# Five TensorE signals per expert instead of ten, and the next expert's transposes behind all down products

## What is computed

```python
h = xf @ W_router + b_router                     # xf: (16384, 128), 32 experts
Sm = softmax(h)
G_ek, idx_ek = top_k(Sm.T, 512)                  # each expert takes its 512 best tokens
tokens = xf[idx_ek]
up = einsum('gjkh,ghf->gjkf', tok_g, W_up) + b_up     # 8 groups of 4 experts, 341 hidden
act = silu(up)
Eout = einsum('ekf,efh->ekh', act, W_down) + b_down
y = zeros.at[idx_ek].add(G_ek[..., None] * Eout)
```

## Time and profile before

| | us |
|---|---|
| median of 3 runs | 2606.75 |
| lowest, highest | 2601.83, 2608.33 |
| the profiled execution | 2612.21 |
| its span, first to last instruction | 2610.5 |
| TensorE busy | 2309.8 |
| VectorE busy | 1869.5 |
| ScalarE busy | 1692.1 |
| POOL busy | 1419.6 |

### The profile page before, as it was taken

One profiled execution on the slowest core, in us unless ns is written; L12 is line 12 of the kernel. 1 busy time (PEld: TensorE's weight loads), 2 busy tenths in 40 slices (PEclk: granted clock), 3 DMA queues, 4 the chain that ended last, 5 costly groups with the idle time before them and its releaser, 6 DMA issues.

```text
span 2610.5 us, 59252 instructions
## 1 busy us (share of the span) xinstructions
PE 2309.8 (88%) x16748; PEld 2017.1 (77%) x16764; DVE 1869.5 (72%) x8460; ACT 1692.1 (65%) x5249; POOL 1419.6 (54%) x1724
## 2 busy tenths in 40 slices
PE   4999977667777599999999999999999999999966
PEld 3877865444444499999999999899898999999855
DVE  4787767555445278888888887777778888788733
ACT  2777744122112287777787777888787888778744
POOL 6544100556556368778887774344443677447443
PEclk8999989888888799999999999999999999999988
DMA  2566686333333431111111126555554888468577
GB/s 74 195 234 209 222 213 97 101 109 122 112 118 117 131 94 50 46 46 43 48 51 46 46 75 170 156 161 163 156 154 110 242 231 243 133 194 243 147 218 226
DMA packets 357908, 361.96 MB, mean 139 GB/s; under 512 B 35603, under 2 KB 301692, under 8 KB 357584
## 3 DMA queue, kind: packets, MB, share of 16 engines
q1 hardware_dynamic: 321376, 272.95, 37.9%
q0 software_dynamic: 33472, 78.98, 9.2%
q10 hardware_dynamic: 2736, 6.25, 0.7%
HBM read 208.38 MB, written 144.00 MB: 135 GB/s over the span
## 4 chain that ended last, share of the span: by engine, by line
PE 64%; DVE 15%; issue 7%; another core or an unknown queue 4%; POOL 3%; ACT 3%; DMA 2%; ACTq 0%; SPq 0%; DVEq 0%; POOLq 0%
PE bank L2210 7%; PE bank L2289 6%; PE bank L2303 6%; PE bank L2221 5%; PE bank L2209 4%; PE bank L2236 4%; PE bank L2256 4%; PE bank L2238 4%; PE bank L2237 4%; PE bank L2264 3%; PE bank L2178 3%; PE bank L2084 2%; POOL rows L910 2%; PE bank L2162 2%
## 5 line engine op out<-in xcount | busy, mean ns | idle before, releaser
L948 POOL DMA_INDIRECT zbuf<-pc,kb x248 | 251.7, 1015 | 242.6 <-DVE pc L1863 189.7
L942 POOL DMA_INDIRECT spread_rows<-kb,pos x248 | 253.7, 1023 | 199.6 <-DVE pc L1863 105.1
L2210 PE MATMUL bank<-xT,gT 128*128 128x256 f32 x1024 | 306.1, 381 | 0.0
L1666 DVE COPY pr_place<-bank 128x384 f32<-128x384 f32 x512 | 281.6, 550 | 19.6 <-PE bank L2221 13.8
L1645 DVE TENSOR_REDUCE nmax<-bank 128x1 f32<-128x128 f32 x512 | 144.1, 282 | 195.8 <-PE bank L2210 108.9
L1153 ACT ACTIVATE pr_place<-bank,nmax 128x128 f32<-128x128 f32 x512 | 188.8, 369 | 136.4 <-DVE nmax L1646 122.6
L2303 PE MATMUL bank<-wvo_part,x_part 128*128 128x512 f32 x768 | 267.8, 457 | 1.1 <-ACT vo_place L1241 1.0
L1163 ACT ACTIVATE bank<-causal 128x384 f32<-128x384 f32 x512 | 253.4, 495 | 19.4 <-PE bank L2394 3.3
L2221 PE MATMUL bank<-ident,pr_place 128*128 128x128 f32 x1536 | 251.8, 273 | 9.9 <-DVE pr_place L1666 9.1
L2221 PEld LDWEIGHTS bank<-ident,pr_place 128*128 128x128 f32 x1536 | 196.9, 140 | 77.1 <-DVE pr_place L1659 14.5
L2289 PE MATMUL bank<-x_part,wqk_part 128*128 128x256 f32 x1536 | 245.8, 296 | 1.2 <-DVE x_part L1806 1.2
(11 more groups left out here) (363 smaller groups left out, 6570.2 us busy)
## 6 DMA issues: line engine op xcount, KB each, us to landing
pa<-bundle SPq DMA_DIRECT2D x196, 321.0 KB
table<-rows SPq DMA_DIRECT2D x96, 576.0 KB
rows<-table SPq DMA_DIRECT2D x192, 128.0 KB
wu_more<-bundle SPq DMA_DIRECT2D x65, 321.0 KB
kb<-spread_rows SPq DMA_DIRECT2D x248, 65.0 KB
junk<-zbuf SPq DMA_DIRECT2D x31, 512.0 KB
h3buf<-h SPq DMA_DIRECT2D x64, 128.0 KB
kb<-kb SPq DMA_DIRECT2D x31, 256.0 KB
```

What stands on the lines that cost most here:

```text
L942: pool.indirect_dma_start(out=spread_rows, out_offset=bass.IndirectOffsetOnAxis(ap=pos[:, k, j:j + 1], axis=0), in_=xr4s[g % 2][:, k, j], ...
L948: pool.indirect_dma_start(out=zbuf, out_offset=bass.IndirectOffsetOnAxis(ap=xu_at(t)[:, C + 1:XW].bitcast(U32), axis=0), in_=yu[:, t % YR] ...
L1666: dve.tensor_copy(prT[:, h % 2], t_bank(u)[:, 0:3 * P]).then_inc(prT_ready, 1)
L2210: pe.matmul(s2[:, P:3 * P], g[:, P:2 * P], xT3[:, p], start=False, stop=True, skip_group_check=True)\
```

## The change

- Up: one signal behind the third product; ScalarE waits once per expert.
- Down: chunks 0 and 1 lie in bank 4 and share a signal, chunks 2 and 3 in bank 7. Each pair waits for the weighing of the pair of the expert before in its bank. Weighing and SyncE's reload count two signals per expert.
- Rows: no signal (but for the first two experts and the last). `number(e + 2)` waits for the signal of bases(e + 3), which TensorE issues behind it. `rank(e + 3)` moves ahead of `number(e + 2)` on VectorE.
- TensorE's order for expert e becomes: turn_rows(e); two warm products; three ups; rows(e + 2); bases(e + 3); four warm products; down 0 to 3.
- The second layer's waits on the two counters take the new totals.

```diff
--- before.py
+++ after.py
@@ -205,7 +205,7 @@
             return w2d[x // 4][:, x % 4, k * C:(k + 1) * C]
 
         def down_at(c):
-            return bank[7 if c % 2 else 4][:, (c // 2) * P:(c // 2 + 1) * P]
+            return bank[7 if c // 2 else 4][:, (c % 2) * P:(c % 2 + 1) * P]
 
         def xg_at(g):
             return xg[:, g % 8] if g % 8 < 4 else xg_more[:, g % 8 - 4]
@@ -559,6 +559,7 @@
         FILLED = NK - 2
         DENSE = (ND + 1) * 2 * H1 + 13
         UPS, DOWNS = 3 * E0, TG * E0
+        UPS_TOLD, DOWNS_TOLD = E0, 2 * E0
         DENSE_STEP = 6
         DENSE_END = DENSE + DENSE_STEP * (E1 - 1) + 1
 
@@ -653,7 +654,7 @@
 
                 for q in range(2 if last else 4):
                     e, p = 4 * v + q, q % 2
-                    sp.wait_ge(dn_mm, TG * (e + 1))
+                    sp.wait_ge(dn_mm, 2 * (e + 1))
                     load_up(v + q // 2, p)
                     load_down(e + 2, p)
             for v in range(0, NU - 1):
@@ -1126,8 +1127,8 @@
                 act.wait_ge(bup_ready, 4 + 2 * v)
                 for q in range(4):
                     e = 4 * v + q
+                    act.wait_ge(up_mm, e + 1)
                     for k in range(3):
-                        act.wait_ge(up_mm, 3 * e + k + 1)
                         act.activation(ac[0:FCH[k], k], bank[1 + k][0:FCH[k], :], ACT.Silu, bias=bupg[0:FCH[k], k:k + 1])\
                             .then_inc(ac_ready, 1)
                     if not (last and q == 3):
@@ -1197,9 +1198,9 @@
 
             def dense_hidden(x):
                 for k in range(2):
-                    act.wait_ge(up_mm, UPS + 2 * x + k + 1)
+                    act.wait_ge(up_mm, UPS_TOLD + 2 * x + k + 1)
                     if x >= 2 and k == 0:
-                        act.wait_ge(dn_mm, DOWNS + x - 1)
+                        act.wait_ge(dn_mm, DOWNS_TOLD + x - 1)
                     act.activation(hd_at(x, k), bank[SBANK[k]][:, :], ACT.Relu, bias=b1T[:, x, k:k + 1]).then_inc(ac_ready, 1)
 
             def dense_gates_turned():
@@ -1543,7 +1544,10 @@
 
             def number(e, q, n):
 
-                dve.wait_ge(tab_mm, e + 1)
+                if 2 <= e < E0 - 1:
+                    dve.wait_ge(base_mm, e + 2)
+                else:
+                    dve.wait_ge(tab_mm, min(e + 1, 3))
                 n.done(dve.tensor_copy(tbase[:].rearrange("p (k c) -> p k c", k=2)[:, 0], bank[5][:, 0:2 * (P + 1)].rearrange("p (c t) -> p c t", c=2)[:, :, P]))
                 n.done(dve.tensor_copy(tbase[:].rearrange("p (k c) -> p k c", k=2)[:, 1], bank[6][:, 0:2 * (P + 1)].rearrange("p (c t) -> p c t", c=2)[:, :, P]))
                 n.wait()
@@ -1570,7 +1574,7 @@
             def weigh(e, p):
                 for c in range(TG):
                     acc = rows4[:, e % NTAB, c, ROW:ROWA]
-                    dve.wait_ge(dn_mm, TG * e + c + 1)
+                    dve.wait_ge(dn_mm, 2 * e + c // 2 + 1)
                     dve.scalar_tensor_tensor(out=acc, in0=down_at(c), scalar=gate[:, p, c:c + 1], in1=acc,
                                              op0=ALU.mult, op1=ALU.add).then_inc(ye_ready, 1)
 
@@ -1587,11 +1591,12 @@
                 n = Steps(dve, sel_step, pre + 4 * PER * v)
                 for q in range(4):
                     e, p = 4 * v + q, q % 2
+                    if not (last and q >= 1):
+                        rank(e + 3, n)
                     if not (last and q >= 2):
 
                         number(e + 2, (q + 2) % 4, n)
                     if not (last and q >= 1):
-                        rank(e + 3, n)
                         place(e + 3, n)
                     gates(e, p, n)
                     weigh(e, p)
@@ -1742,7 +1747,7 @@
                     dve.wait_ge(mask_ready, NG)
                 else:
                     dve.wait_ge(ye_ready, DOWNS + x)
-                dve.wait_ge(dn_mm, DOWNS + x + 1)
+                dve.wait_ge(dn_mm, DOWNS_TOLD + x + 1)
                 hh = h3[:].rearrange("p q j c -> p (q j) c")
                 for j in range(TG):
                     ins = dve.scalar_tensor_tensor(out=yd[:, j], in0=dense_bank(x)[:, j * C:(j + 1) * C], scalar=gmat[:, j, x:x + 1],
@@ -1751,7 +1756,7 @@
 
             def dense_biases():
                 dve.wait_ge(ye_ready, DOWNS + E1)
-                dve.wait_ge(dn_mm, DOWNS + E1 + 1)
+                dve.wait_ge(dn_mm, DOWNS_TOLD + E1 + 1)
                 dve.tensor_tensor(xeT[:], dense_bank(E1)[:, :], xeT[:], ALU.add).then_inc(ye_ready, 1)
 
             def gate_weights(g):
@@ -2131,7 +2136,8 @@
                 for c in range(TG):
                     o = bank[5 + c // 2][:, (c % 2) * (P + 1):(c % 2 + 1) * (P + 1)]
                     ins = pe.matmul(o, oneh[:, c * P:(c + 1) * P], tab[:], start=True, stop=True)
-                ins.then_inc(tab_mm, 1)
+                if e < 2 or e == E0 - 1:
+                    ins.then_inc(tab_mm, 1)
 
             pe.wait_ge(tq_ready, 1)
             for e in range(3):
@@ -2153,32 +2159,31 @@
             def serve(v, last):
                 for q in range(4):
                     e, p = 4 * v + q, q % 2
-                    if not (last and q >= 2):
-                        rows(e + 2)
+                    turn_rows(e)
                     stay_warm(3, 2)
                     pe.wait_ge(xeT_ready, e + 1)
                     pe.wait_ge(wup_in[p], 16 * (2 * v + q // 2 + 1))
                     for k in range(3):
-                        pe.matmul(bank[1 + k][0:FCH[k], :], wup[:, p, k * P:k * P + FCH[k]], xeT[:], start=True, stop=True)\
-                            .then_inc(up_mm, 1)
-                        if k == 1 and not (last and q >= 1):
-                            bases(e + 3)
-                    stay_warm(0, 3)
+                        ins = pe.matmul(bank[1 + k][0:FCH[k], :], wup[:, p, k * P:k * P + FCH[k]], xeT[:], start=True, stop=True)
+                    ins.then_inc(up_mm, 1)
+                    if not (last and q >= 2):
+                        rows(e + 2)
+                    if not (last and q >= 1):
+                        bases(e + 3)
+                    stay_warm(0, 4)
                     pe.wait_ge(ac_ready, 3 * e + 3)
                     pe.wait_ge(wdn_in[p], 48 * (2 * v + q // 2 + 1))
                     for c in range(TG):
-                        if c == 1 and not (last and q >= 1):
+                        if c == 2 and not (last and q >= 1):
                             pe.wait_ge(base_read, e + 4)
-                        if c == 2 and not (last and q == 3):
-                            turn_rows(e + 1)
-                        if TG * e + c >= 2:
-                            pe.wait_ge(ye_ready, TG * e + c - 1)
+                        if c % 2 == 0 and e >= 1:
+                            pe.wait_ge(ye_ready, TG * (e - 1) + c + 2)
                         for k in range(3):
                             m = FCH[k] + (k == 2)
                             ins = pe.matmul(down_at(c), ac[0:m, k, c * P:(c + 1) * P], wdn[0:m, p, k],
                                             start=(k == 0), stop=(k == 2))
-                        ins.then_inc(dn_mm, 1)
-            turn_rows(0)
+                        if c % 2:
+                            ins.then_inc(dn_mm, 1)
             serve(0, False)
             for v in range(1, NU - 1):
                 serve(v, False)
```

## The result

| | before | changed |
|---|---|---|
| median | 2607.54 us (4 runs) | 2654.01 us (4 runs) |
| lowest, highest | 2601.83, 2620.23 | 2644.88, 2664.47 |
| profiled execution | 2612.21 | 2664.47 |
| ratio, 95% interval | | 1.0171 [1.013, 1.0212] |

A forecast was written before the change was run, and what follows sets the result against it. A two-expert loop of waits bounds the expert stage. Leg 9.05 + 1.8 + 0.9 = 11.75, with 13.11 on POOL, gives period 12.43 against 13.19: 0.76 x 31 = 23.6 us gained, near 2583; range 2549 to 2609.

The forecast's parts named there:

- The bound and the loop of two legs: First layer's expert stage: a chain of waits over two experts, 13.84 us on TensorE plus 13.11 on POOL, sets the period.
- POOL leg: From first weighing of expert e to transposes of e+2, eight indirect transfers included: 13.11 us, expected unchanged.
- (1): Up products: three signals become one, so the first silu waits for all three; 1.7 us head start lost, cost 0.
- (2): Down products: four signals become two, pairs in one bank; first weighing waits 0.67 us longer, cost 0 under the same cover.
- VectorE's branch: Number, place and gate up to the first weighing, at 9.05 us; ends 1.0 after the silu and down branch at 8.05.
- (4): Rank before number, rows and bases behind the ups: third up product no longer held up; later index costs 0.
- (3): Transposes of e+1 move behind down product 3: last two products, weighings and scatters freed; e+1's chain needed them anyway.
- The lateness taken: Late signals on the TensorE leg: 0.5 us for transposes, 1.9 for base product, in three of four experts: 1.8 us.
- Prompt leg 9.05: From transposes to first weighing in the changed kernel, at full clock with prompt signals: 9.05 us.
- Half clock share kept at 24%: TensorE at half clock for today's share of the stage lengthens 3.9 us of work on the leg by 0.9 us.
- Slower: Rival: TensorE's own serial loop becomes the bound, 13.9 us per expert, +22 us, 2629 us; chance 0.14.
- Signals turn prompt: Rival: fewer TensorE signals no longer queue, period 11.1 to 12.1, gain 65 to 34 us, time 2542 to 2573; chance 0.18.

The follow-up runs named there:

- e4: The kernel before with only the signal counts and banks changed: one signal for three ups, two for four downs; ratio 1.0082 to before.
- e1: The changed kernel with the transposes put back between down products 1 and 2; ratio 0.9968 to before.
- e18: The changed kernel with a short break on POOL, a fill of 160 columns, ahead of scatter 2; ratio 0.9948 to before.
- e2: The kernel before with only the transposes moved behind down product 3; ratio 1.0102 to before.
- e8: The kernel before with a signal nobody waits for on each of the seven warm products per expert; ratio 1.0019 to before.
- e16: The changed kernel with each scatter replaced by a gather of the same rows into an idle tile, sums left out; one execution, 2622.80 us.
- e6: The changed kernel with six warm products instead of two between the transposes and the ups; ratio 1.0003 to before.
- e12: The kernel of e6 with six warm products instead of two also behind the downs, before the wait for the gather; ratio 1.0006 to before.
- e15: The changed kernel with a break on POOL, a fill of 1284 columns, ahead of scatter 2; ratio 0.9991 to before.

## Why the prediction was wrong

- **The bound and the loop of two legs**: right, but it closes over the even experts alone. Their leg is 16.2 us in the mean and their POOL leg 13.2, half the sum 14.7, against a measured period of 14.74. The odd experts have 10.0, where the prediction has both "alike"; their transposes follow TensorE's own downs, and their POOL leg of 19.3 sets nothing.
- **(1), (2) signals at cost 0 under VectorE's branch**: right only with the new order. Alone they cost 0.8% (e4).
- **(4) order**: right in sign. The predicted 2583 would have been -0.9% for all parts; the order alone gave -0.4%, with the signals -0.3% (e1).
- **(3) the transposes' move**: this failed, in two sentences. "What now stands behind them is expert e+1's own chain, which needed them anyway: 0" looked only at what waits for the transposes, not at what TensorE does behind them. In the kernel before twelve down matmuls followed at once and the copy came 0.15 us late in the mean; now only two warm products follow, and it came 2.46 us late, in 13 experts over 1 us, up to 9.5. In the even experts, which close the loop, that is 4.7 us, where 0.75 x 0.5, about 0.4, was taken. It is the largest addition to their leg of 16.2: 9.05 prompt, 4.7 for the held signal, and some 2.3 more than in odd experts for transposes and ups at the lower clock.
- **The lateness taken**, "0.5 and 1.9": the 1.9 stood on the base product's signal, the 0.5 on the transposes'. The trace has it the other way round. In expert 12 the base product ends at 650.79 and number starts at 650.84, and in the mean it starts 0.1 us behind; the transposes' signal is the late one, and so, in front of each of the 13 late copies, is the last down signal. The upper bound, "as late as the worst seen: 1.46 and 2.26", was no bound: the kernel before shows no signal in front of an idle TensorE in a long run of POOL's but the down signal of chunk 1, late by 2.9 us (725.17 to 728.06), and even that was counted as "the next 2 us behind it", a queue.
- **Prompt leg 9.05**: right where signals are prompt and the clock is full. The odd experts of e18 have 8.9, its even ones, behind the stand for the gather, 10.6.
- **Half clock share kept at 24%**: it rose to 36% (granted clock 0.82), as TensorE's stands grew (1.09 us of work in 9.60 in the window above, at 0.56). The term taken was 0.9 us; the 2.3 above stand against it.
- **Rivals.** "Slower" had the sign but not the mechanism: it has TensorE's own loop as the bound and no stand for gathered rows, and TensorE stood for them 17 times, 52.6 us. Its path is the one that e2 took. "Signals turn prompt" by number has e8 against it: more of them cost nothing. The Trainium skill ("TensorE: Matmul & The Clock Gate", section "The cost: per-tile semaphore tail") gives some 26 ns per increment, for products of small tiles that run side by side. An estimate by it: e8's seven more would be 0.18 us per expert if all lay on the loop. The period stayed at 13.19, so e8 shows no such price and only bounds it from above. The rule does not cover the holding beside POOL's runs, 8.1 us in expert 12.

## What to carry to other kernels

A signal that a whole chain waits for should not be moved to where TensorE stands idle behind it and POOL is in a dense run of indirect transfers, unless that is measured: here the same transposes cost 1.0% (e2) to 2.0% (changed against e1) more behind the down products than between them. When a signal in the profile is seen late ("remote", "issue"), look at what its engine and POOL do between the event and the wake-up before a price is put on it, look at every waiter of every signal and not at one, and take a change of position as a new case that the old trace doesn't bound. Read such a loop by even and odd experts: a mean over both hid that all 13 late copies were in even experts. A break of about a microsecond in POOL's run took the changed kernel from 1.0171 to 0.9948, and gave the kernel before nothing, so it is worth a trial and no rule.

## What the runs showed of the hardware

- Beside unbroken runs of indirect transfers on POOL (about 1.0 us each, 0.30 apart) signals of TensorE reach the waiting engine up to 9.5 us after the product's modelled end, and two waiting engines see the same signal at the same time (637.21 in expert 12). With one break of 1.06 us in each expert's eight (e18) the transposes' signals come in 0.04 us and the down signals in 0.1 in the mean.
- Neither a larger number of signals (e8) nor writes to HBM (e16) are needed to make them late. More work behind the transposes made the copies less late (2.46 to 0.78 us in e6) and the last down signal late in more experts (16 to 22).
- A held signal can arrive in the middle of a run of POOL's (9 of 13 in the changed kernel), 1.4 to 1.7 us after its end (24 of 26 first weighings in e12), and later than a stand of 0.9 us (4 of 13).
- Open: what path the signal and POOL's transfers share; whether it is their issuing or their being under way, since no run has one without the other; what SyncE's weight transfers, issued by the signal just ahead, add. They are under way in the prompt experts and in e15 and e18 too, so they can't hold it alone. How short a break still serves was not tried below 1.06 us. Lateness can only be read from profiled executions, so how large it is in one without a profile is not shown.
